# Turning the gathered tokens at the head of a step: a Mamba and expert kernel on one core

## The reference

```python
xn = layernorm(x)
x = x + mamba(xn) + experts(xn)

def mamba(x):
    x_ssm, x_gate = split(x @ in_proj_w.T + in_proj_b)
    x_conv = silu(causal_conv4(x_ssm) + conv_b)
    B, C = split(x_conv @ bc_w.T + bc_b)            # 16 states
    dt = softplus(x_conv @ dt_w.T + dt_b)
    # for each token: h = h * exp(dt * A) + dt * B * x_conv ; y = h . C + x_conv * D
    y = scan(...) * silu(x_gate)
    return layernorm(y @ out_w.T + out_b + x) * ln_g + ln_b

def experts(x):                                      # 4096 tokens, 8 experts, hidden size 1024
    logits = silu(x @ rw1 + rb1) @ rw2 + rb2
    w = softmax over the 2 largest logits of a token
    return x + sum over the 2 experts e of w[e] * (silu(x @ we1[e] + be1[e]) @ we2[e] + be2[e])
```

## Time and profile before

| | |
|---|---|
| median of 3 runs | 936.59 us (936.52 to 938.7) |
| profiled execution, its own time | 936.73 us |
| its span, first to last instruction | 934.3 us |
| busy: TensorE, VectorE | 787.8 us, 787.8 us (84% each) |
| busy: ScalarE, GpSimd | 664.3 us (71%), 601.2 us (64%) |
| mean granted TensorE clock | 0.961 of 2.4 GHz |

### The profile page before, as it was taken

The page is one execution under the profiler, slowest core; times in us unless marked ns, Lnnn a source line. Parts: engine busy times, 40 slices in busy tenths (PEclk is TensorE's granted clock), DMA queues, the critical chain, the costliest instruction groups (busy, mean ns, idle before and its releaser), DMA issues.

```text
span 934.3 us, 14382 instructions
## 1 busy us (share of the span) xinstructions
PE 787.8 (84%) x4533; PEld 634.1 (68%) x4533; DVE 787.8 (84%) x774; ACT 664.3 (71%) x1134; POOL 601.2 (64%) x384
## 2 busy tenths in 40 slices
PE   3993669978998899888989899889989997899852
PEld 2662647857776677677876777677768786778741
DVE  6818839798889968998899698989899889989993
ACT  1433668777688768876886878886878788869930
POOL 3571515757477757876767756884787487758861
PEclk9996989999999999999999999999999999999985
DMA  9939437568566865797668775786577667877731
GB/s 298 389 142 345 173 109 242 138 205 272 180 209 199 255 222 187 209 278 217 212 203 241 238 239 152 233 273 203 185 219 256 215 210 222 244 226 228 227 90 22
DMA packets 81927, 201.00 MB, mean 215 GB/s; under 512 B 7936, under 2 KB 41216, under 8 KB 81728
## 3 DMA queue, kind: packets, MB, share of 16 engines
q1 hardware_dynamic: 61424, 171.46, 53.4%
q0 software_dynamic: 19168, 26.59, 14.9%
q10 hardware_dynamic: 1264, 2.05, 0.7%
HBM read 174.38 MB, written 26.61 MB: 215 GB/s over the span
## 4 chain that ended last, share of the span: by engine, by line
DVE 36%; PE 27%; ACT 10%; issue 9%; DMA 6%; SPq 1%; POOL 1%; DVEq 0%; ACTq 0%; POOLq 0%
DVE ps_drive L935 13%; PE ps_up L1229 11%; DVE ring L942 9%; DVE ps_drive L928 7%; PE ps_yx L1243 6%; DMA bc_scratch<-sp 6%; PE ps_fr L1160 5%; ACT L787 3%; DVE xx L909 2%; ACT da L760 2%; PE ps_fr L1185 1%; PE ps_up L1223 1%; SPq L524 1%; DMA out<-yo,sid 1%; PE ps_up L1288 1%
## 5 line engine op out<-in xcount | busy, mean ns | idle before, releaser
L592 POOL TENSOR_TENSOR y<-y,ring 128x1024 f32<-128x1024 f32 x126 | 325.5, 2583 | 59.1 <-ACT y L751 51.8
L935 DVE TENSOR_TENSOR_SCAN ps_drive<-da,ps_drive 128x1024 f32<-128x1024 f32 x128 | 293.7, 2295 | 41.5 <-ACT da L760 37.8
L1229 PEld LDWEIGHTS ps_up<-xgt,w1s 128*128 128x128 f32 x2272 | 284.7, 197 | 17.9 <-issue 9.6
L1229 PE MATMUL ps_up<-xgt,w1s 128*128 128x128 f32 x2272 | 284.6, 280 | 0.0
L1243 PE MATMUL ps_yx<-w,ht 128*128 x1136 | 270.7, 382 | 0.0
L1243 PEld LDWEIGHTS ps_yx<-w,ht 128*128 128x128 f32 x1136 | 206.4, 192 | 28.8 <-issue 5.0
L581 POOL DMA_INDIRECT out<-yo,sid x71 | 117.9, 1660 | 147.0 <-ACT yo L802 107.6
L787 ACT ACT_TABLE_LOAD x143 | 183.5, 1283 | 2.5
L760 ACT ACTIVATE da<-gd,col 128x511 f32<-128x511 f32 x256 | 168.3, 710 | 0.0
L928 DVE TENSOR_TENSOR ps_drive<-ps_u,rep 128x1024 f32<-128x1024 f32 x128 | 157.4, 1229 | 9.5 <-DVE ring L942 0.5
L942 DVE TENSOR_TENSOR ring<-ps_drive,rep 128x1024 f32<-128x1024 f32 x128 | 156.5, 1223 | 3.9
(11 more groups left out here) (161 smaller groups left out, 724.1 us busy)
## 6 DMA issues: line engine op xcount, KB each, us to landing
w1s<-in_we SPq DMA_DIRECT2D x71, 1024.0 KB, 7.3
rep<-bc_scratch SPq DMA_DIRECT2D x128, 512.0 KB, 4.4
w<-in_we SPq DMA_DIRECT2D x8, 1024.0 KB, 11.9
w<-in_x SPq DMA_DIRECT2D x8, 512.0 KB, 11.0
xn_scratch<-da SPq DMA_DIRECT2D x8, 512.0 KB, 7.2
out<-w POOLq DMA_DIRECT2D x8, 512.0 KB, 6.2
xnt_scratch<-xx SPq DMA_DIRECT2D x8, 512.0 KB, 5.7
xx<-xnt_scratch SPq DMA_DIRECT2D x8, 512.0 KB, 3.3
```

Source lines behind the costliest of these rows:

```text
L592: pool.tensor_tensor(y[:, :, :], y[:, :, :], ring[:, g % RING, :, :], ALU.add).then_inc(s_sum, 1)
L935: dve.tensor_tensor_scan(states, da[:, g % DECAYS, :, :].rearrange("p k l -> p (k l)"), states, 0.0, ALU.mult, ALU.add).then_inc(s_scanned, 1)
L1229: mm = pe.matmul(bank[:, c * P:(c + 1) * P], w1s[:, q, k, at:at + P], xgt[:, k, :], start=False, stop=(c == 3 and k == KD - 1))
```

## The change

At the steps 2 to 8, `turn_x(s+2)` moves on TensorE to the head of the step, ahead of `up` of tile s+1. It writes the bank `fr` and not up0, and waits for its gather, for the last reader of `fr`, and for the copy of the tile before. On ScalarE `copy_x(s+2)` moves from behind the Exp table load to behind the SiLU table load, ahead of the two SiLU passes. `xgt` gets a second buffer, so the copy waits only for `up` of the tile two before it. Each later use of `fr` also waits until the turned tokens are copied (`bank_free`). The turns of the steps 0 and 1 stay where they were.

```diff
--- before.py
+++ after.py
@@ -105,7 +105,7 @@
         y = sb("y", [P, KD, L])
         xtok = sb("xtok", [P, TB, D])
         xg = sb("xg", [P, 2, D])
-        xgt = sb("xgt", [P, KD, P])
+        xgt = sb("xgt", [P, 2, KD, P])
         rep = sb("rep", [P, REPS, 2, L])
         kbuf = rep[:, 0, :, :].rearrange("p r l -> p (r l)")
         th = rep[:, 1, :, :].rearrange("p r l -> p (r l)")
@@ -494,6 +494,12 @@
             uses.append(("out", b, 0))
         front = {use: n for n, use in enumerate(uses)}
 
+        def at_head(j):
+            return j >= 2 and (j - 2) % STEPS >= 2
+
+        def turned(j):
+            return psum["fr"][:, 0:D] if at_head(j) else tr_x
+
         def positive(n):
             return not isinstance(n, int) or n > 0
 
@@ -762,9 +768,9 @@
 
                 def copy_x(j):
                     act.wait_ge(s_x_turned, j + 1)
-                    if positive(j):
-                        act.wait_ge(s_up_ready, j * 2)
-                    act.activation(xgt[:, :, :], tr_x.rearrange("p (k c) -> p k c", k=KD), ACT.Copy).then_inc(s_x_copied, 1)
+                    if j >= 2:
+                        act.wait_ge(s_up_ready, j * 2 - 2)
+                    act.activation(xgt[:, j % 2, :, :], turned(j).rearrange("p (k c) -> p k c", k=KD), ACT.Copy).then_inc(s_x_copied, 1)
 
                 def weights_in(n):
                     q = n % 2
@@ -824,6 +830,8 @@
                         ln_dt(b + 1)
                     if s + 1 < MT:
                         table_of(ACT.Silu)
+                        if s + 2 < MT and at_head(s + 2):
+                            copy_x(s + 2)
                         for h in range(2):
                             hidden(s + 1, h)
                     if i in (0, 1):
@@ -844,7 +852,7 @@
                     table_of(ACT.Exp)
                     if i == 3 and b > 0:
                         seed_exp(b - 1)
-                    if s + 2 < MT:
+                    if s + 2 < MT and not at_head(s + 2):
                         copy_x(s + 2)
                     if i + 1 < IN:
                         decay(b, i + 1, 1)
@@ -1152,10 +1160,18 @@
 
             @block.tensor
             def _(pe):
-                def project(at, rows_out, f, src):
-
+                used = [0]
+                last_turned = [0]
+
+                def bank_free(f):
                     if positive(f):
                         pe.wait_ge(s_fr_read, f)
+                    if last_turned[0] > 0:
+                        pe.wait_ge(s_x_copied, last_turned[0])
+                    used[0] = f + 1
+
+                def project(at, rows_out, f, src):
+                    bank_free(f)
                     for k in range(KD):
                         mm = pe.matmul(psum["fr"][0:rows_out, :], wm[:, k, at:at + rows_out], src[:, k, :],
                                        start=(k == 0), stop=(k == KD - 1))
@@ -1175,7 +1191,7 @@
 
                 def proj_out(b, half):
                     pe.wait_ge(s_y_gated, b + 1)
-                    pe.wait_ge(s_fr_read, front["out", b, half])
+                    bank_free(front["out", b, half])
                     for c in range(2):
                         j = 2 * half + c
                         dst = psum["fr"][:, c * D:(c + 1) * D]
@@ -1189,7 +1205,7 @@
                 def last_out(j):
                     pe.wait_ge(s_y_gated, B + j // 2)
                     if j == 0:
-                        pe.wait_ge(s_fr_read, front["out", B - 2, 1] + 3)
+                        bank_free(front["out", B - 2, 1] + 3)
                     if j in (1, 2):
                         pe.wait_ge(s_hidden, 2 * MT)
                     if j == 3:
@@ -1203,10 +1219,14 @@
 
                 def turn_x(j):
                     pe.wait_ge(s_gathered[j % 2], j // 2 * 16 + 16)
-                    if positive(j):
+                    if at_head(j):
+                        pe.wait_ge(s_fr_read, used[0])
+                        pe.wait_ge(s_x_copied, j)
+                        last_turned[0] = j + 1
+                    elif j > 0:
                         pe.wait_ge(s_hidden, j * 2 - 1)
                     for k in range(KD):
-                        mm = pe.transpose(tr_x[:, k * P:(k + 1) * P], xg[:, j % 2, k * P:(k + 1) * P], ident[:, :])
+                        mm = pe.transpose(turned(j)[:, k * P:(k + 1) * P], xg[:, j % 2, k * P:(k + 1) * P], ident[:, :])
                     mm.then_inc(s_x_turned, 1)
 
                 def expert(j):
@@ -1226,7 +1246,7 @@
                     for c in range(4):
                         at = (4 * h + c) * P
                         for k in range(KD):
-                            mm = pe.matmul(bank[:, c * P:(c + 1) * P], w1s[:, q, k, at:at + P], xgt[:, k, :],
+                            mm = pe.matmul(bank[:, c * P:(c + 1) * P], w1s[:, q, k, at:at + P], xgt[:, j % 2, k, :],
                                            start=False, stop=(c == 3 and k == KD - 1))
                     mm.then_inc(s_up_ready, 1)
 
@@ -1248,6 +1268,8 @@
 
                     s = b * STEPS + i
                     prepare = b < B - 1
+                    if s + 2 < MT and at_head(s + 2):
+                        turn_x(s + 2)
                     if s + 1 < MT:
                         up(b, i + 1, e_next, 0)
                     if i == 0 and b > 0:
```

## The result

The changed kernel takes 1109.74 us (median of 6 runs, 1098.97 to 1116.7) against 937.64 us for the kernel before on the same chip: ratio 1.181, 95% interval 1.177 to 1.185. It is slower, as predicted, but by 172 us and not by 60. The profiled execution took 1109.33 us for a span of 1107.2. Times are medians of all executions; the ratios and their intervals leave out executions over 1.5% above the fastest of the same kernel.

The account below looks back on a forecast made before the run. The lead passes between VectorE, TensorE and ScalarE, by way of the B/C write. Six periods at +9.4 give 56.4, first batch 3.6, last 0: 60.0 on 936.7 gives 997 us, range 958 to 1016 (8 in 10).

Parts of the forecast that it names:

- Point 1: Head of step 2: TensorE waits 3.9 us for the gather, 4.2 with semaphore and turn; 25.6 us over seven batches.
- Point 2: Projections of steps 2, 3, 5, 6 wait for `copy_x` on ScalarE; second SiLU pass of step 3 6.5 us late.
- Step 6 of the walk: Last softplus read of step 6 at 421.4 us against 412.39; the projection chain takes the lead from the B/C write.
- the walk: Time-by-time account of one batch period from the first scan at 334.67: 108.0 us instead of 98.6, +9.4; chance 0.62.
- The walk's second such term: Step 8: the last gather lands 3.9 us after issue, at 434.7; 2.7 to 8.3 moves the sum −7 to +26.
- The clock: Rival: TensorE's clock falls at idles of steps 2 and 5, 1.5 us each, 18 in all: 1015 us; chance 0.12.
- The last batch has slack: 0: Last batch, with no projections and VectorE's alone: its late turns have slack and cost 0 us.
- First batch: First batch: no LayerNorm of a predecessor on ScalarE and a smaller landing wait; adds 3.6 us.
- The rival "faster": Rival: landings don't bind; first scan 2.0 us earlier in each of seven batches, 14 in all: 923 us; chance 0.05.
- Only the landing counts: Rival: projection waits are absorbed, only gather landings at step 2 cost, 27.7 us: 964 us; chance 0.17.
- B: Theory of the follow-up experiments: projections wait for the bank of the turned tokens, that is for `copy_x`.

## Why the prediction was wrong, step by step

The direction was right, and so was the reading that the projections come to wait for `xgt` and the turns for gathers, and that the taps' wait grows (8.89 us in the period, where about 7 was predicted). The size was a third of the real one, outside the range.

*Point 1, the wait at step 2:* right. 3.86 us in the period (3.9 predicted), and as the only head moved 24.6 us of waits in the seven batches against 25.6. The trace sided with the rows and not with the Trainium skill's "DMA: Bandwidth & Descriptors", section "Anatomy of one DMA — SWDGE (gpsimd) path": by its figures these 128 KB take about 2.3 us, an estimate; here they took 6.7 at this place, and 2.7 to 11.9 in all.

*Point 2, the projections' waits:* right in kind and place. It is the main wait as soon as the gathers are out of the way (78.3 us), and first scans are then (879.72 − 235.32) / 6 = 107.4 us apart. In the kernel after, it mostly hides under the gathers' waits.

*Step 6 of the walk, the step that failed.* The walk let the copy of step 6 start when ScalarE was free, at 416.45, and so took it that TensorE's turn was there in time, with no gather wait at all. The turn came at 423.2, after a wait of 7.06 us; the last softplus read was 11.0 us behind the walk. Two things were missing. The issue: by the walk's own `weigh` of step 4 (396.6, against 391.11) it would come near 401.33 + 5.5 = 406.8, an estimate; it came at 447.60 − 36.03 = 411.6. And the landing: 11.6 us instead of 6.0, because the gather, once late, meets a 1 MB load of another queue.

The walk's second such term is the landing of the last gather, step 8. Its bound (2.7 to 8.3 us, 434.7) was wide enough for the landing of 8.3, but the issue was 11 us late too. A single landing of 3.9 was read from one period; the trace of before already held 7.5 and 8.3 at this place, in the periods where the load goes out 1.01 and 0.25 us behind the gather. Holding the weight loads back gives both gathers the old landings, and takes 78 of the 113 us between forecast and result.

A small slip stands beside it: the walk ends 442.7 − 432.72 = 10.0 us later than this period really did, but was counted as 9.4, against the average period of 98.6. That is 3.5 us in six periods.

*The clock:* taken as a rival with two falls a period, 1.5 us each. It falls behind the gather waits of steps 2, 5, 6 and 8, and in four of seven batches behind the copy wait of 2.58 us at step 3 (0.61 to 0.64 over the next 4 us; 1.00 in the other three). Filling the waits gave back 35 us, against 18. The Trainium skill's "TensorE: Matmul & The Clock Gate", section "HAM oscillation — how this bites in real kernels", says that groups of matmuls parted by waits for DMA start at half clock each time. The trace agrees for the gather waits, in part for those of 2.58 us, and does not for the copy waits of 1.72 and 1.77 us in the kernel with three buffers. The length of the wait alone does not decide it either: with step 2 alone at the head, six copy waits of 1.87 us were followed by a mean clock of 0.63 to 0.67 three times and of 1.00 three times. The 78 and the 35 us were measured apart and overlap: with the loads held, the clock is 0.927 already.

*"The last batch has slack: 0":* wrong by 7.9 us. *First batch:* 12.8 us against 3.6, the same causes.

*The rival "faster"* gave 923 us, and the kernel with three buffers and the early copy takes 925 and 927. Its condition, that the landings don't bind, is not met by this change. The agreement of the numbers is partly luck: the rival has a first scan 2.0 us earlier in each batch by what happens at its end, and in that kernel a period is 1.0 us shorter; with three buffers and the heads of the steps 4, 7 and 8 alone, which should show it, 934 us remain. Where the gain comes from is open.

*"Only the landing counts"* fell: B costs 53 us with no gather wait at all.

Taken away in this order, of the 172 us: 119 go with the gathers (the meetings with the weight loads and the falls of the clock behind gather waits lie within them), then 65 with the copy's place, and 12 of gain are left once both are out of the way. Taken first, the copy's place is worth 37 to 44.

## What to carry to other kernels

A landing time read from a trace holds for the order of issues in that trace. When a change makes one queue late, look which transfers of another queue its own now meet, just ahead or just behind, and price the landing with them. The spread of a landing in the trace of before is worth a look for that: sort it by the distance to the nearest big transfer. And before a wait is put at the head of an in-order engine, follow it round: if what it waits for is issued by work that depends on the last head, its price can be more than the wait. Here a third buffer, and a copy ahead of the other work on ScalarE, turned +18% into −1.2%.

## What the runs showed of the hardware that I had not expected

- A gather of 128 KB lands after 2.7 to 11.9 us. Issued 0.28 us behind a 1 MB load, and 1.7 us behind a 512 KB store, it took 11.6; with the load held behind it, 5.9. A load issued 0.25 us behind the gather also counts (8.3 us, against 2.8 to 4.9 with 1.5 us or more between them).
- A wait costs TensorE more than its length: 16 matmuls of `up` took 3.33 us behind a wait of 3.86 us, and 1.95 us further on. Working through the waits gave back 35 us, though it added matmuls.
- Costs of moved heads do not add: 41, 24 and 20 us apart, 172 us together.
